# Attention twice over eight images: a third pair of superblocks by transposes, and the residual base held as token rows

## What is computed

```python
g = group_norm(x)                                   # 32 groups
e = (Wq g + bq)^T (Wk g + bk)                       # 2304 x 2304
x = x + gamma * (Wv g + bv) softmax(e)^T + g * sigmoid(w2 relu(w1 mean(g)))
t = tokens(x)                                       # 2304 x 128
a = layer_norm(t)
t = t + softmax(a a^T) a
u = layer_norm(t)
t = t + top2_of_8_experts(u)                        # gates from softmax(u @ router_w + router_b)
```

## Time and profile before

| | |
|---|---|
| median of 3 runs | 2571.59 us (2570.17 to 2571.62) |
| the profiled execution | 2570.53 us |
| its span, first to last instruction | 2568.8 us |
| mean granted TensorE clock | 0.997 |
| TensorE busy | 2511.7 us, 98%, 15057 matmuls |
| VectorE busy | 2118.4 us, 82% |
| ScalarE busy | 1812.1 us, 71% |
| POOL busy | 451.3 us, 18% |
| DMA | 23.10 MB, mean 9 GB/s |
| mirrored slots | 90 in the kernel (12 per image, 6 in the last) |

### The profile page before, as it was taken

One profiled execution on the slowest core, in us unless ns is written; L12 is line 12 of the kernel. 1 busy time (PEld: TensorE's weight loads), 2 busy tenths in 40 slices (PEclk: granted clock), 3 DMA queues, 4 the chain that ended last, 5 costly groups with the idle time before them and its releaser, 6 DMA issues.

```text
span 2568.8 us, 45236 instructions
## 1 busy us (share of the span) xinstructions
PE 2511.7 (98%) x15057; PEld 2309.8 (90%) x15057; DVE 2118.4 (82%) x6229; ACT 1812.1 (71%) x3542; POOL 451.3 (18%) x839
## 2 busy tenths in 40 slices
PE   6999999999999999999999999999999999999997
PEld 5889998999988999899998999899998999989996
DVE  6886888878888788887888878888779887898677
ACT  4767766677667776777767777677776777667775
POOL 0000221012210131101311013010240112300135
PEclk9999999999999999999999999999999999999999
DMA  1000000000000000000000000000000000000000
GB/s 40 1 19 1 4 10 1 23 4 7 8 3 20 4 7 8 23 1 4 10 4 23 1 4 10 4 22 2 4 10 4 22 1 4 13 1 4 1 10 13
DMA packets 11317, 23.10 MB, mean 9 GB/s; under 512 B 1360, under 2 KB 7760, under 8 KB 11088
## 3 DMA queue, kind: packets, MB, share of 16 engines
q1 hardware_dynamic: 11088, 20.20, 2.2%
HBM read 10.76 MB, written 9.44 MB: 8 GB/s over the span
## 4 chain that ended last, share of the span: by engine, by line
PE 74%; DVE 16%; ACT 6%; issue 3%; POOL 0%; DMA 0%; ACTq 0%; DVEq 0%; SPq 0%; POOLq 0%
PE ps L1178 21%; PE ps L1180 20%; PE ps L1179 20%; PE ps L1198 10%; DVE row_space L977 4%; DVE pt_lo L992 4%; ACT row_space L731 2%; PE ps L1323 1%; DVE pt_lo L1072 1%; ACT pt_hi L742 1%; DVE gn_raw L854 1%; ACT row_space L783 1%; DVE pt_lo L1077 1%; ACT row_space L828 0%; DVE t_tok L1015 0%
## 5 line engine op out<-in xcount | busy, mean ns | idle before, releaser
L742 ACT ACTIVATE pt_hi<-ps 128x384 fp32r<-128x384 f32 x864 | 417.1, 489 | 282.8 <-PE ps L1198 282.1
L992 DVE TENSOR_TENSOR pt_lo<-ps,pt_hi 128x384 fp32r<-128x384 f32 x864 | 473.5, 551 | 119.2 <-ACT pt_hi L742 116.4
L977 DVE TENSOR_SCALAR_CACHE_REDUCE row_space<-ps,key_bias 128x512 f32<-128x512 f32 (+1 forms) x720 | 492.7, 689 | 47.8 <-PE ps L1180 46.9
L731 ACT ACTIVATE row_space<-row_space,negmax 128x512 f32<-128x512 f32 (+2 forms) x432 | 403.1, 933 | 89.0 <-DVE negmax L986 88.0
L1198 PE MATMUL ps<-ident,row_space 128*128 128x128 f32 x2736 | 444.2, 273 | 3.7 <-ACT row_space L731 3.7
L1198 PEld LDWEIGHTS ps<-ident,row_space 128*128 128x128 f32 x2736 | 346.9, 141 | 73.6 <-ACT row_space L731 5.9
L1178 PE MATMUL ps<-pt_hi,v_hi 128*128 128x384 f32 x864 | 352.7, 408 | 13.9 <-DVE pt_lo L992 6.7
L1077 DVE TENSOR_TENSOR pt_lo<-row_space,pt_hi 128x768 fp32r<-128x768 f32 x260 | 251.2, 967 | 96.1 <-ACT pt_hi L792 96.0
L783 ACT ACTIVATE row_space<-ps,shift 128x768 f32<-128x768 f32 x260 | 234.2, 901 | 128.7 <-PE ps L1180 127.4
L1178 PE MATMUL ps<-pt_hi,tn_hi 128*128 128x384 f32 x864 | 303.4, 351 | 1.5 <-DVE pt_lo L1077 0.5
L1180 PE MATMUL ps<-pt_hi,v_lo 128*128 128x384 f32 x864 | 292.9, 339 | 0.0
(11 more groups left out here) (207 smaller groups left out, 5376.0 us busy)
## 6 DMA issues: line engine op xcount, KB each, us to landing
x_chan<-x SPq DMA_DIRECT2D x24, 384.0 KB, 4.1
y<-acc SPq DMA_DIRECT2D x48, 192.0 KB, 1.9
t_tok<-eb SPq DMA_DIRECT2D x1, 516.0 KB, 5.6
t_tok<-ew SPq DMA_DIRECT2D x1, 516.0 KB, 6.4
row_space<-wqkv SPq DMA_DIRECT2D x1, 192.0 KB, 3.3
se_sb<-se SPq DMA_DIRECT2D x1, 68.0 KB, 4.9
biases<-channel SPq DMA_DIRECT2D x1, 2.0 KB, 5.2
```

Source lines behind the costliest of these rows:

```text
L731: act.activation(part, part, ACT.Exp, bias=negmax[:, r:r + 1], accum_out=dparts[:, n, r, u:u + 1]).then_inc(p_rows_ready, 1)
L742: act.activation(pt_hi[:, slot, :], ring_bank(step)[:, 0:BW], ACT.Copy)\
L977: dve.tensor_scalar(row_part(n, r, a, w), ring_bank(step)[:, 0:w], key_bias[:, row:row + 1], None, ALU.add, ALU.max, accum_out=mx[:, row % ...
L992: dve.tensor_tensor(pt_lo[:, slot, :], ring_bank(step)[:, 0:BW], pt_hi[:, slot, :], ALU.subtract).then_inc(pt_lo_ready, 1)
```

## The change

1. Superblock 2 takes superblock 0's exponentials too: slots 36 to 41 are mirrored in images 0 to 6 (18 of 54 slots), from the exponentials of slots 12 to 17. These are kept in `x_chan`, in two late pieces of a score row's buffer and in a place shared by `o_chan` and `tn_tok`.
2. For that, x can't be needed any more when the second attention runs. The base is made in token rows: the host also hands x over by tokens, SP loads it into `t_tok` in two parts, and POOL multiplies by a row of scales and adds a row of shifts. The rows come from `spread` (VectorE copies the two columns to 128 x 128 each), two transposes (`rows`) and a ScalarE copy. The steps `base` and the transposes and copies of `baset` go.
3. The third early score row moves from slots 25 to 31 to slots 30 and 42 to 47, its exponentials to slots 49 to 53, since its buffer now holds kept pieces.
4. Tables are changed: block 4's router goes to (1, 16), its gates to (2, 1); blocks 0 to 3 are shifted by some slots; the row sums of block 4 go to slot (6, 2), behind the evacuation; in (6, 4) the product goes ahead of the transposes; the statistics of the next image shift by a slot.
5. In the last image the experts of block 4 go to slots 57 to 62, behind the last residual sum. The last block has buffers of its own for u, the terms of block 4 three places, and the last tile is summed by VectorE in place of POOL.
6. The ring of PSUM banks is put in another order once per image, late in the first attention.

```diff
-EARLIER_BLOCK = {1: {11: [('uln',)], 12: [('uapply',)], 15: [('ut',)]}, 2: {8: [('router',)], 10: [('gates',)]},
+EARLIER_BLOCK = {1: {8: [('uln',)], 10: [('uapply',)], 13: [('ut',)], 16: [('router',)]}, 2: {1: [('gates',)]},
...
-BASE_TILES = {(1, 9): [0], (2, 10): [1], (3, 9): [2], (3, 12): [3], (4, 10): [4], (4, 12): [5]}
+BASE_TILES = {(1, 9): [0], (2, 6): [1], (3, 6): [2], (4, 6): [3], (5, 6): [4], (5, 14): [5]}
...
-    values_lead = n >= 2 and j < 2
+    values_lead = n >= 2 and j < 2 or n == NB and j == 4
...
+    if n == 1 and j == 5:
+        s.append(("rows", b, 0))
...
-        s += [(kind, b, n - 2) for kind in ("rowsum", "ln", "lnapply", "lnhigh", "lnlow") if j == L0_SLOTS[kind]]
+        s += [(kind, b, n - 2) for kind in ("rowsum", "ln", "lnapply", "lnhigh", "lnlow")
+              if j == (2 if kind == "rowsum" and n == NB else L0_SLOTS[kind])]
...
-MOE_SLOTS = [(6, 9, 11, [13, 13, 15, 16, 17, 18]), (22, 25, 26, [28, 28, 31, 31, 32, 33]), (31, 34, 35,
-             [37, 38, 39, 40, 41, 42]), (39, 42, 43, [45, 45, 46, 46, 47, 47]), (44, 48, 49, [50, 51, 51, 52, 52, 54])]
-O1_SLOTS = [20, 29, 38, 40]
+MOE_SLOTS = [(6, 9, 11, [13, 13, 15, 16, 17, 18]), (22, 25, 26, [28, 28, 29, 30, 31, 32]), (29, 33, 34,
+             [36, 36, 37, 38, 38, 39]), (40, 43, 44, [46, 46, 47, 48, 49, 49]), (45, 50, 51, [52, 53, 53, 53, 54, 54])]
+O1_SLOTS = [20, 27, 38, 40]
...
-                  [48, 48, 49, 49, 50, 50]), (48, 51, 52, [53, 53, 54, 54, 55, 55]), (56, 59, 61,
-                  [62, 62, 63, 64, 65, 65])]
+                  [48, 48, 49, 49, 50, 50]), (48, 51, 52, [57, 57, 58, 60, 60, 62]), (56, 59, 61,
+                  [63, 63, 64, 64, 65, 65])]
...
-EARLY_SLOTS = [([12, 14, 15, 16, 17], 17, [20, 21, 23]), ([21, 21, 23, 23, 24], 25, [25, 26, 29]), ([25, 26, 27, 27, 30], 31,
-               [32, 34, 37])]
+EARLY_SLOTS = [([12, 14, 15, 16, 17], 17, [20, 21, 23]), ([21, 21, 23, 23, 24], 25, [25, 26, 29]), ([30, 42, 44, 45, 47], 47,
+               [49, 51, 53])]
...
+    if 2 * TPS <= w < 3 * TPS and b + 1 < B:
+        return w - 2 * TPS, 2
...
+    if 2 * NT <= w < 2 * NT + TPS and b + 1 < B:
+        return w - 2 * NT, 2
...
+            if which == 2:
+                late = (p_rows[:, ROW_BUFFER[2, 0], LW:2 * LW], p_rows[:, ROW_BUFFER[2, 0], 2 * LW:3 * LW], spare[:, :])
+                return x_chan[:, t * LW:(t + 1) * LW] if t < LB else late[t - LB]
...
+                if kind == "baset":
+                    m = step[2]
+                    t = t_tok[:, TPB * m:TPB * (m + 1), :]
+                    shape = [128, TPB, 128]
+                    pool.wait_ge(base_rows_ready, at(base_rows_ready, "rows", b, 0))
+                    pool.wait_ge(tokens_loaded[m // 4], 16 * (b + 1))
+                    pool.tensor_tensor(t, t, base_rows[:, 0, :].unsqueeze(1).broadcast_to(shape), ALU.mult)\
+                        .then_inc(base_scaled, 1)
+                    pool.wait_ge(base_scaled, at(base_scaled, *step))
+                    pool.tensor_tensor(t, t, base_rows[:, 1, :].unsqueeze(1).broadcast_to(shape), ALU.add)\
+                        .then_inc(base_tok_ready, 1)
...
+                    sp.wait_ge(expert_added, at(expert_added, "expert", b, 3, TPB - 1))
+                    load_tokens(b + 1, 0)
+                    sp.wait_ge(o1_added, at(o1_added, "o1add", b, NB - 1))
+                    load_tokens(b + 1, 1)
                     store(b, 4)
...
-                    act.activation(x_chan[:, cols], x_chan[:, cols], ACT.Identity, bias=yshift, scale=yscale)\
-                        .then_inc(base_done, 1)
...
+                elif step == LAST_TILE:
+                    m, k = step[2:]
+                    term = [term_of(b, m, k, i) for i in range(5)]
+                    total = acc[:, m % 2, k, :]
...
+                    dve.wait_ge(vector_chain, chained(step, links[0]))
+                    dve.tensor_tensor(total, total, term[0], ALU.add).then_inc(tile_added, 1)
```

More of the change, by code:

```diff
@@ L316, with ring_order @@
 RING = list(ORDER["ring_full"])
+def ring_order(left):
+    order = [0, 1, 2, 3, 4, RING0, RING0 + 1]
+    turn = -left % len(order)
+    return order[turn:] + order[:turn]
 def ring_banks():
@@ L324, in ring_banks @@
     had, bank, before = {}, {}, {}
+    ring_index = {step: i for i, step in enumerate(RING)}
+    ordered = -1
     for step in PLAN:
         kind, b = step[0], step[1]
+        if kind == "pt" and step[2] in (2, 3) and ordered < b:
+            left = ring_index["pt", b, NB - 1, NT - 1] + 1 - ring_index[step]
+            if not set(free[-3:]) & set(ring_order(left)[:2]):
+                free, ordered = ring_order(left), b
         if (kind, step[-1]) == ("s1", 0):
@@ L460, in build @@
         xg_lo_ready = signal("xg_lo_ready")
-        base_done = signal("base_done")
+        rows_spread = signal("rows_spread")
+        base_rows_ready = signal("base_rows_ready")
+        base_scaled = signal("base_scaled")
+        tokens_loaded = [signal(f"tokens_loaded{i}") for i in range(2)]
         fused_hi_ready = signal("fused_hi_ready")
@@ L645, in take @@
                     pool.tensor_tensor(ln_rs[:, :], ln_ve[:, :], minus_half[:, :], ALU.pow).then_inc(ln_rstd_ready, 1)
-                if kind == "scaled":
+                if kind == "scaled" and step != LAST_TILE:
                     m, k = step[2:]
-                    term = [term_of(m, k, i) for i in range(5)]
+                    term = [term_of(b, m, k, i) for i in range(5)]
                     total, paired = acc[:, m % 2, k, :], at(terms_paired, *step) * 4 - 4
@@ L920, in take @@
                     dve.wait_ge(vector_chain, chained(step, links[0]))
+                elif kind == "spread":
+                    if b:
+                        dve.wait_ge(ring_full, filled(("rows", b - 1, 0)))
+                    dve.tensor_copy(rows_src[:, :, :], gs[:, 9:11].unsqueeze(2).broadcast_to([128, 2, 128])).then_inc(rows_spread, 1)
                 elif kind == "xgnorm":
@@ L1166, in take @@
                     ins.then_inc(expert_added, 1)
+                elif step == LAST_TILE:
+                    m, k = step[2:]
+                    term = [term_of(b, m, k, i) for i in range(5)]
+                    total = acc[:, m % 2, k, :]
+                    dve.wait_ge(expert_added, at(expert_added, "expert", b, m, k))
+                    link(dve.tensor_tensor(total, total, term[4], ALU.add))
+                    dve.wait_ge(terms_ready, at(terms_ready, *step))
+                    link(dve.tensor_tensor(term[0], term[0], term[1], ALU.add))
+                    link(dve.tensor_tensor(term[2], term[2], term[3], ALU.add))
+                    dve.wait_ge(vector_chain, chained(step, links[0]))
+                    link(dve.tensor_tensor(term[0], term[0], term[2], ALU.add))
+                    dve.wait_ge(vector_chain, chained(step, links[0]))
+                    dve.tensor_tensor(total, total, term[0], ALU.add).then_inc(tile_added, 1)
                 assert links[0] == linked(step), (kind, links[0])
@@ L1260, in take @@
                     ins.then_inc(ring_full, 1)
-                elif kind == "baset":
-                    m = step[2]
-                    pe.wait_ge(base_done, at(base_done, "base", b, m // 2))
-                    transpose3(step, lambda k: x_chan[:, m * BW + k * 128:m * BW + (k + 1) * 128])
+                elif kind == "rows":
+                    wait_ring(step)
+                    pe.wait_ge(rows_spread, at(rows_spread, "spread", b))
+                    for k in range(2):
+                        ins = pe.transpose(ring_bank(step)[:, k * 128:(k + 1) * 128], rows_src[:, k, :], ident[:, :])
+                    ins.then_inc(ring_full, 1)
                 elif kind == "score":
@@ L1362, in take @@
                         out = ring_bank(step)[:, k * 2 * E:(k + 1) * 2 * E]
-                        pe.matmul(out, u_lo[:, tile], rw_pair[:, :, :], start=True, stop=False)
-                        ins = pe.matmul(out, u_hi[:, tile], rw_pair[:, :, :], start=False, stop=True)
+                        pe.matmul(out, u_low(b, m)[:, tile], rw_pair[:, :, :], start=True, stop=False)
+                        ins = pe.matmul(out, u_high(b, m)[:, tile], rw_pair[:, :, :], start=False, stop=True)
                     ins.then_inc(ring_full, 1)
```

93 lines of the change are left out of this document (54 added, 39 removed).

## The result

The changed kernel takes 2586.39 us (median of 4 runs, 2584.66 to 2588.89) against 2571.61 before (4 runs beside it): ratio 1.006, 95% interval 1.0048 to 1.0073. It is slower by 14.8 us, where 34.6 less were forecast. The profiled execution took 2587.91 us with a span of 2586.2, 17.4 over the span in the earlier trace rows.

A forecast was written before the change was run, and what follows sets the result against it. TensorE, busy 98% of the span, was taken as the bound, with VectorE next at 82%. The terms summed to -34.6 us from 2570.5, and 1.1 more against the median gave 2537; range 2524 to 2556.

The forecast's parts named there:

- part 6: Slots 36 to 53: full VectorE costs 3.5 us, the third early row's exponentials on ScalarE 2.5 us.
- Part 2: Base in token rows: removed transposes save 11.8 us, first image saves 1; added transposes cost 1.6, POOL's work 1.
- Part 3: Last block row, n=6: row sums after the evacuation let the copy of the sums start earlier, 5.2 us saved.
- Part 4: Block 4's router one block row earlier, n=2 to n=1: 4 us saved, ends 8 saved and 6 lost.
- Part 1: Slots 36 to 41 mirrored, 42 slots in seven images: 0.40 us each if nothing waits, 15.7 us saved.
- Parts 2 and 5: Part 2, plus the last block with experts moved behind and last tile on VectorE: 5.5 us saved for the latter.
- A: Slots 36 to 53: VectorE, then ScalarE, set the pace; 15 us less gained, 2552, up to 2558; chance 0.22.
- B: POOL's new work delays VectorE: 26 us at 0.27 each, or 65 us (2602); chance 0.04.
- C: Slots 36 to 47: TensorE's clock falls in the long run of transposes, up to 2754; chance 0.02.
- E: Slots 12 to 17 wait because kept places come free too late; 2544 at 1 us per image; chance 0.01.

The follow-up runs named there:

- e11: e10 with the third early score row in the changed kernel's late slots (30, 42, 44, 45, 47; exponentials 49, 51, 53): 2557.38 us, ratio 0.9952.
- e10: e8 with block 1's experts in slots 36, 36, 37, 38, 38, 39 instead of 37 to 42: 2542.74 us, ratio 0.9887.
- e3: e2 plus the third pair (slots 36 to 41 mirrored) and the late third early row: 2572.71 us, ratio 1.0007.
- e7: e2 plus the third pair of mirrored slots, with the third early row left in slots 25 to 31: 2564.71 us, ratio 0.9973.
- e5: e2 with the third early row and its exponentials in the changed kernel's late slots, no third pair: 2587.11 us, ratio 1.0057.
- e1: Changed kernel with block 1's residual sum and its transposes back in slot 29 instead of 27: 2574.37 us, ratio 1.0012.
- e6: e1 with block 4's router and gates, the row sums and the statistics back where the kernel before had them: 2571.65 us, ratio 0.9999.
- e12: e2 with e10's slots for block 1 (norm, transposes, router, experts) and no third pair: 2562.84 us, ratio 0.9968.
- e2: Changed kernel with the earlier kernel's tables and slots 36 to 41 computed; base in token rows and last block's changes stay: 2556.11 us, ratio 0.994.
- e8: e7 with block 1's norm, transposes and router at slots 30, 33, 34 instead of 31, 34, 35: 2552.03 us, ratio 0.9925.

## Why the prediction was wrong

**The step that failed** is part 6, "What comes back", together with a term that was never written. Part 6 named the third early row and priced *its exponentials on ScalarE* (2.5 us). It did not price its five score chunks, four of which went with it into slots 42 to 47: there they can be the third step of a slot on a ring of two banks. The exponentials, which it did price, cost nothing: slots 48 to 52 take 15.4 us with them (e11) and without (e10). The row as a whole cost 8.0 us beside the pair with the old slots (e3 against e7), 14.6 in good ones (e11) and 31 without the pair (e5). And the moves of the residual sum (29 to 27) and of the experts of blocks 0 to 3 had no term, not even "nothing, as this hides it". The first alone cost 12.0 (e1), the second some 14 (e6 against e11). Part 2 named a cover for the DMAs and for POOL; the tables got none.

The four steps of the table above are 43.6 us. The prediction had -3.2 for them (parts 3 and 4 at -9.2, part 6 at +6.0). The difference, 46.8, is all but 2.6 of the 49.4 us between the forecast of -34.6 and the measured +14.8.

By the parts of the prediction:

*Part 1, third pair, -15.7.* The work is as forecast: slots 36-41 in e10 and e12 differ by 2.9 us per image, and the six times 0.40 are 2.4 of it. But the time it gives is not one number: 27.5 us gained in the changed kernel's tables, 20.1 in e10's, 8.6 *lost* in those of before (e2 to e7). "If nothing waits" was the condition, and it held only after a router was moved by a slot.
*Parts 2 and 5, base in token rows (-10.2 with its additions) and last block (-5.5).* Together -15.7 forecast, -15.3 measured (e2). That they agree so well is in part luck. The last block by itself is over-sized: from the start of slot 53 of the last image to the end the changed kernel takes 3.2 us less than the one before, and e2 3.6, not 5.5. So some 12 of the 15.3 are the base's, for which 10.2 were forecast. POOL's instructions took less than estimated, as the group of the changed kernel shows:

```profile
L703 POOL TENSOR_TENSOR t_tok<-t_tok,base_rows 128x384 f32<-128x384 f32 x48 | 48.8, 1016 | 47.5 <-DMA t_tok<-tokens 47.5
```

1.02 us each, not 1.35. POOL waits for the load of the tokens, but no group of TensorE's in e2 waits for POOL.

*Part 3, row sums behind the evacuation, -5.2:* failed. The wait for the copy was removed (0.2 us left of 6.6), and one of 0.68 for the low half came up behind the norm; "the next thing late would be the copy itself" named the wrong successor.
*Part 4, block 4's router, -4:* failed. n=1 took 28.20 instead of 27.30 and n=2 27.50 instead of 28.40: what one gained the other lost. The text had seen that "the same wait can arise", and bet against it: it is the one behind the router in e6's section. Parts 3 and 4 together were -9.2 forecast and +2.7 measured (e6, which moves the statistics back with them).
*Part 6, VectorE "full" in slots 36 to 47, +3.5.* Its busy time is no guide. e7 waited 15.3 us there with VectorE at 82% of the stretch; e10 has it at 94% (14.51 of 15.40) in slots 36-41, and TensorE is busy for all of the 15.40.

Put the failed steps at what e10 has of them, parts 1, 2 and 5 alone: 2570.5 - 15.7 - 10.2 - 5.5 + 1.1 = 2540.2. e10 took 2542.7. That is close, again with some luck: the pair and its slots gained 13.4 over e2, for 15.7. But the sum of what was removed was sound; the cost of the moves made for it was what the change was really about.

**The rivals.** A had part of the place (slots 36 to 53; the largest single wait stands in slot 28), but at most 2558, and a cause that e8 to e10 exclude: in slots 36 to 41 neither VectorE nor ScalarE is the bound. B falls as the loss: e2 has all of POOL's new work and took 2556.1, where B asked for 2575 or more (e2's expectation). VectorE's low half took as long as before, over all 864, in the changed kernel:

```profile
L1052 DVE TENSOR_TENSOR pt_lo<-ps,pt_hi x864: 534/551/561, 45.9 to 2413.8; 128x384 fp32r<-128x384 f32 x173
```

But what the prediction worked out for a normalisation that meets a step of POOL's did happen. In seven images of the changed kernel the first normalisation of block 4's u begins 0.1 us after POOL's second instruction of the base and ends 0.1 us after it:

```profile
1008.76 1.02 POOL L706 TENSOR_TENSOR t_tok<-t_tok,base_rows 128x384 f32<-128x384 f32 x1
...
1008.87 1.50 DVE L1108 TENSOR_SCALAR u_tok<-t_late,u_mv,u_rs 128x128 f32<-128x128 f32 x3
...
L1108 DVE TENSOR_SCALAR u_tok<-t_late,u_mv,u_rs x48: 332/343/984, 373.2 to 2568.9; 128x128 f32<-128x128 f32 x48
```

It takes 0.98 us, not 0.34: 0.64 more at one per image, where the prediction had up to 1.35. In e2, where this step stands two slots later, none of the 48 takes over 0.50. It is 4.5 us of VectorE in all; how much of it reached TensorE, no run shows.

C falls: the granted clock is 1.00 in both stretches of mirrored slots, twelve in a row, in all seven images of the changed kernel and of e10, so what the Trainium skill (TensorE: Matmul & The Clock Gate, Part 4: PE-mode transpose) says of transposes costs this kernel nothing, with real matmuls between them. No run here shows E: slots 12 to 17 took 20.5 us in images 1 to 6, as before. The chance of 0.05 for slower was spent on mechanisms of the hardware; the one that happened was in the schedule.

## What to carry to other kernels

When a change shifts entries of a schedule to make room, give each shift a term, and read it from the queue of the engine in between: what stands ahead of the instruction that frees the buffer, and how many steps of the slot share the buffers. Ask this anew for every part that gets faster, since TensorE then arrives earlier at the same queue: e7's router was harmless at 2.8 us per slot and cost 15 us of waiting at 2.4. And where a wait on a nearly full engine goes, look for it a few slots on before counting it as saved.

## What was not expected of the hardware

After the 1.8 us wait in e5 the granted clock fell from 1.00 to 0.50, the lower of its two levels (1.2 GHz), and stood there for about 3.4 us (1277.3 to 1280.6). It did so in six of the seven images. In the seventh the same wait left it at 1.00, and slots 42 to 47 took 22.3 us instead of 23.9:

```profile
2215.43:2237.69 22.26, 19.39 (x116) 16.74 (x114) 18.56 (x57) 10.10 (x25) 8.46 (x19) 1.00 0.03 10
```

The wait of 2.24 us in slot 28 of the changed kernel left it at 1.00 in four images, image 3 among them, and was followed by 0.50 in the other three, where slots 28 and 29 took 10.3 to 10.5 us instead of 8.9:

```profile
906.05:916.34 10.29, 8.05 (x37) 7.15 (x36) 6.76 (x22) 5.80 (x11) 2.01 (x5) 0.83 0.00 0
```

So one and the same wait in one execution costs 1.4 to 1.6 us more, or nothing more. What TensorE did just before does not tell the cases apart: it was busy for 0.34 of the 1.50 us ahead of the fall in e5, and for none of the 1.50 us from 1228.50 to 1230.00 in image 3 of the changed kernel, where the clock stayed. What does, no run here settles.
